# Moving transposed-tile copies from VectorE to ScalarE, joining two copies, and reordering the last pass of a transformer layer

## The reference

```
def _L0_attn_ref(src, ...):
    Q = elu(src @ Wq + bq) + 1 ;  K = elu(src @ Wk + bk) + 1 ;  v = src @ Wv + bv
    KV = einsum('bshd,bshm->bhdm', K, v)
    Z = 1.0 / (einsum('bshd,bhd->bsh', Q, K.sum(axis=1)) + EPS)
    o = einsum('bshd,bhdm,bsh->bshm', Q, KV, Z)
    x = LN(src + o @ Wo + bo, g1, be1)
    y = gelu(x @ W1 + b1) @ W2 + b2
    return LN(x + y, g2, be2)
def _L0_ffn_ref(x, weight, disha):
    pooled = x.reshape(..., 1024 // 64, 64).sum(axis=-2)
    return x @ weight.T + pooled @ disha
x = x + _L0_attn_ref(LN(x), ...)
x = x + _L0_ffn_ref(LN(x), weight, disha)
```

## Time and profile before

| what | value |
|---|---|
| runs shown | 2300.01 and 2508.72 us, median 2404.36 us |
| profiled execution, its time | 2298.4 us |
| profiled execution, span of its slowest core (core 2) | 2296.9 us |
| spans of the eight cores | 2281.9 to 2296.9 us |
| granted clock of TensorE, mean of each core | 0.903 to 0.907 |
| busy: PE, DVE, ACT, POOL | 1867.8, 687.0, 697.9, 218.3 us |

### The profile page before, as it was taken

The page is one execution under the profiler, slowest core; times in us unless marked ns, Lnnn a source line. Parts: engine busy times, 40 slices in busy tenths (PEclk is TensorE's granted clock), DMA queues, the critical chain, the costliest instruction groups (busy, mean ns, idle before and its releaser), DMA issues.

```text
span 2296.9 us, 36221 instructions; the slowest of 8 cores (2281.9 to 2296.9 us)
## 1 busy us (share of the span) xinstructions
PE 1867.8 (81%) x12660; PEld 1109.0 (48%) x12850; DVE 687.0 (30%) x1115; ACT 697.9 (30%) x1326; POOL 218.3 (10%) x186
## 2 busy tenths in 40 slices
PE   3888878887857777499999999999999999477766
PEld 1444444444433333266666666666666666343333
DVE  2232333333237777400000000000000000376674
ACT  1333333333323333223222222222222222233222
POOL 6000000000002222200000000000000000222220
PEclk9999999998978888699999999999999999777777
DMA  9930111111026665401112111110111110245542
GB/s 181 183 89 29 55 38 47 37 47 38 10 84 191 199 184 170 117 24 52 52 51 51 51 51 47 47 25 26 44 47 47 47 47 29 101 149 200 184 165 101
DMA packets 64084, 191.41 MB, mean 83 GB/s; under 512 B 7907, under 2 KB 8036, under 8 KB 62884
## 3 DMA queue, kind: packets, MB, share of 16 engines
q1 hardware_dynamic: 29108, 94.55, 12.6%
q0 software_dynamic: 16368, 35.80, 10.2%
q10 hardware_dynamic: 18432, 58.73, 6.6%
HBM read 166.12 MB, written 58.72 MB: 98 GB/s over the span
## 4 chain that ended last, share of the span: by engine, by line
PE 40%; DVE 13%; DMA 8%; issue 5%; ACT 2%; DVEq 0%; ACTq 0%; SPq 0%; POOL 0%; POOLq 0%
PE psC L920 19%; DVE arena L209 13%; PE psA L932 10%; PE psB L932 10%; DMA arena<-u_s 5%; DMA x_s<-arena 3%; ACT arena L209 2%; PE psB L702 1%; DMA arena<-Wf 0%; PE psA L947 0%; PE psA L1260 0%; DVEq L208 0%; PE psC L1260 0%; DMA arena<-x 0%; ACTq L1034 0%
## 5 line engine op out<-in xcount | busy, mean ns | idle before, releaser
L920 PE MATMUL psC<-arena 128*128 128x256 bf16 x4096 | 540.1, 277 | 18.0 <-DVE arena L209 18.0
L920 PEld LDWEIGHTS psC<-arena 128*128 128x128 bf16 x4096 | 405.2, 99 | 175.7 <-issue 23.8
L209 DVE SCALAR_TENSOR_TENSOR arena<-psA,arena 128x256 bf16<-128x256 f32 (+2 forms) x160 | 93.6, 585 | 1218.4 <-PE psA L947 945.9
L209 ACT ACTIVATE arena<-psC,arena 128x256 bf16<-128x256 f32 x512 | 242.3, 473 | 635.0 <-PE psC L920 629.8
L209 ACT ACTIVATE arena<-arena 128x1 f32<-128x1 f32 (+3 forms) x418 | 248.8, 595 | 350.2 <-DVE arena L209 314.4
L932 PE MATMUL psA<-arena 128*128 128x512 bf16 x960 | 294.3, 383 | 37.0 <-ACT arena L209 34.2
L932 PE MATMUL psB<-arena 128*128 128x512 bf16 x976 | 297.4, 383 | 2.5
L209 DVE SCALAR_TENSOR_TENSOR arena<-arena 128x1024 f32<-128x1024 f32 (+1 forms) x128 | 172.3, 1346 | 104.0 <-DMA arena<-u_s 37.1
L209 DVE TENSOR_SCALAR arena<-arena 128x1 f32<-128x1 f32 (+1 forms) x322 | 179.5, 557 | 73.6 <-ACT arena L209 30.6
L932 PEld LDWEIGHTS psB<-arena 128*128 128x128 bf16 x1024 | 101.0, 99 | 124.2 <-issue 6.0
L554 PE MATMUL psA<-arena 128*128 128x256 bf16 x1024 | 151.1, 297 | 0.0
(11 more groups left out here) (111 smaller groups left out, 1438.3 us busy)
## 6 DMA issues: line engine op xcount, KB each, us to landing
arena<-x SPq DMA_DIRECT2D x96, 512.0 KB, 5.4
x_s<-arena ACTq DMA_DIRECT2D x32, 512.0 KB, 3.9
arena<-x_s SPq DMA_DIRECT2D x32, 512.0 KB, 7.8
u_s<-arena ACTq DMA_DIRECT2D x32, 512.0 KB, 8.6
arena<-u_s SPq DMA_DIRECT2D x32, 512.0 KB, 5.3
out<-arena ACTq DMA_DIRECT2D x32, 512.0 KB, 6.0
arena<-W POOLq DMA_DIRECT2D x32, 256.0 KB, 74.2
qt_s<-arena ACTq DMA_DIRECT2D x32, 256.0 KB, 2.3
```

Of the source, the lines that this page charges most:

```text
L209: inst = fn(*a, **kw)
L920: ii = te.matmul(ph, w1_v[w][:, c * P:(c + 1) * P], x1t[:, w, :], start=(w == 0), stop=(w == NCH - 1))
```

## The change

It has three parts. In pass B1 the two half copies of `sc_VoT` become one of 1024 columns, and `pe_Pat` waits for it before its first matmul. In pass B2a the two copies `cvxt` leave DVE and go to ACT as `scxt`, ahead of and behind `scw`, with the same waits; DVE keeps only `cvu`. In pass B2b `vcols` of a pair is run one pair later, behind that pair's `vg2`, `vout` goes ahead of `vn`, and `ar3` on ACT goes to the head of the next pair.

```diff
@@ pass B1, PE and ACT
-                    W(te, f"bVoTa_{u}")
+                    W(te, f"bVoT_{u}")
...
-                        if w == 4:
-                            W(te, f"bVoT_{u}")
...
-                    sc.copy(oTv[:, 0:512], ps_bf[:, 0:512],
-                            key=f"bVoTa_{u}")
-                    sc.copy(oTv[:, 512:1024], ps_bf[:, 512:1024],
-                            key=f"bVoT_{u}")
+                    sc.copy(oTv[:, :], ps_bf[:, :], key=f"bVoT_{u}")
@@ pass B2a, DVE
                 for st in range(NSUP):
                     if st >= 1:
                         cvu(2 * st - 2)
-                    cvxt(2 * st)
-                    cvxt(2 * st + 1)
-                    if st >= 1:
                         cvu(2 * st - 1)
@@ pass B2a, ACT
+                def scxt(t):
...
+                    sc.copy(x1tv[:, :, sub * P:(sub + 1) * P],
+                            pt.rearrange("p (c s) -> p c s", c=NCH),
+                            key=f"cVxT_{t}")
...
                 for st in range(NSUP):
+                    scxt(2 * st)
                     scw(st)
+                    scxt(2 * st + 1)
                     for c in range(NFCH):
@@ pass B2b, DVE
                     vg2(t)
                     vg2(t2)
                     if p >= 1:
-                        vn(t - 2)
-                        vn(t2 - 2)
+                        vcols(t - 2)
+                        vcols(t2 - 2)
                     if p >= 2:
                         vout(t - 4)
                         vout(t2 - 4)
+                    if p >= 1:
+                        vn(t - 2)
+                        vn(t2 - 2)
                     vxa(t)
                     vxa(t2)
-                    vcols(t)
-                    vcols(t2)
+                vcols(T - 2)
+                vcols(T - 1)
@@ pass B2b, ACT
                     if p >= 1:
+                        ar3(t - 2)
+                        ar3(t2 - 2)
                         nT_(t - 2)
...
                     sq(t)
                     sq(t2)
-                    ar3(t)
-                    ar3(t2)
+                ar3(T - 2)
+                ar3(T - 1)
```

More of the change, by code:

```diff
@@ L957, in _ @@
                 psDbf_v = psD.ap().bitcast(BF16)
-                def cvxt(t):
-                    if t >= T:
-                        return
-                    st = t // 2
-                    sub = t % 2
-                    pt = ps_bf[:, :] if sub == 0 else psDbf_v[:, 0:1024]
-                    W(v, f"cPt_{t}")
-                    W(v, f"cPh_{st - 2}_{NFCH - 1}")
-                    x1tv = x1Ts if st % 2 == 0 else x1Ts2
-                    v.tensor_copy(x1tv[:, :, sub * P:(sub + 1) * P],
-                                  pt.rearrange("p (c s) -> p c s", c=NCH),
-                                  key=f"cVxT_{t}")
                 def cvw(st):
@@ L1014, in scw @@
                                 key=f"cVW_{st}")
+                def scxt(t):
+                    st_ = t // 2
+                    sub = t % 2
+                    pt = ps_bf[:, :] if sub == 0 else psDbf_s[:, 0:1024]
+                    W(sc, f"cPt_{t}")
+                    W(sc, f"cPh_{st_ - 2}_{NFCH - 1}")
+                    x1tv = x1Ts if st_ % 2 == 0 else x1Ts2
+                    sc.copy(x1tv[:, :, sub * P:(sub + 1) * P],
+                            pt.rearrange("p (c s) -> p c s", c=NCH),
+                            key=f"cVxT_{t}")
+                psDbf_s = psD.ap().bitcast(BF16)
                 for st in range(NSUP):
+                    scxt(2 * st)
                     scw(st)
+                    scxt(2 * st + 1)
                     for c in range(NFCH):
```

## The result

The kernel with the change is slower: 1.0251 times the time before, with a 95% interval of 1.0236 to 1.0266, some 58 us. The forecast was 2350 us, 1.022 times the profiled execution before. The medians of all executions, 2447.08 us of 11 with the change and 2303.89 of 10 before, contain, for both kernels, disturbed ones, in which the cores of a die show a lower clock; every ratio here leaves them out, and the other executions of the change lie between 2357.07 and 2360.03 us. The profiled execution took 2360.35 us, 62 more than the one before.

The account below looks back on a forecast made before the run. PE was taken to bound pass B2a, and a ring of DVE work, an SP issue and a DMA pass B2b. B1 0, B2a +55 and B2b -3 gave +52 us on 2298.4: 2350 us, range 2320 to 2385.

Parts of the forecast that it names:

- my number stands against the former: Whole kernel: the forecast is to be compared with the run at 2300.01 us, not the one at 2508.72.
- the clock term: Pass B2a: lower PE clock after longer stops at 15 meetings, 25 us against 13 before: +12, bounds 0 and 25.
- B1, 0 us: Pass B1, joined copies: PE's later start is covered, as DVE doesn't wait for this product: 0 us, from -8 to +14.
- the upper bound of 14 us: Pass B1: PE's first matmul starts 0.43 us later, 32 times, with nothing covering it.
- The waiting term: Pass B2a: `py` 2.35 us later at eight meetings, 3.3 at seven with a weight piece: 42 us.
- Eight matmuls take half of 1.91 us: Pass B2a, meetings: time of the first `ph` products after the stop, leading to `py` at about +9.1.
- the +80 of the pass: Pass B2a together: upper bound of the forecast of +55 us, from +43 to +80.
- B2b, -3 us: Pass B2b, reordering: a pair goes from 17.6 to 17.4 us, over 15 pairs -3 us, from -27 to +22.
- rival 1: Pass B2b: reordering pays fully, pairs fall to 15.8 us, -27 us, B2a's clock no worse: 2314 us; chance 0.20.
- PE's ring: Pass B2b: PE from transposition to last product, plus `vout` and `vn`: no pair can be under 15.8 us.
- Rival 2: Pass B2b: loads gain nothing and column operations take their full price, +22 us: 2375 us; chance 0.22.
- Rival 3: Pass B2a: copies hidden behind PE, the meetings cost nothing: 2295 us, or 2271 with rival 1's gain; chance 0.03.

Follow-up runs that it names:

- run 2: Kernel before with only the change's B2a part, the copies moved to ACT: 2361.65 us, ratio 1.0259 to the kernel before.
- run 4: Whole change, but on ACT the copies of the next super tile stand ahead of the two squares and stores: 2319.65 us, 1.0076 to the kernel before.
- run 7: The change's B1 and B2b, but B2a's copies stay on DVE, behind both `cvu`: 2301.39 us, 0.9994 to the kernel before.
- Run 1: Kernel before with only the change's B1 part, the joined copy: 2306.94 us, ratio 1.0014 to the kernel before.
- run 5: Whole change, with PE's stops at B2a's meetings filled by matmuls whose product nobody reads: 2331 to 2345 us, 1.0164 to the kernel before.
- Run 3: Kernel before with only the change's B2b part, the new order: 2302.72 us, ratio 1.0003 to the kernel before.
- run 6: Whole change, with the square of the mean in `vcols` as TENSOR_SCALAR instead of TENSOR_TENSOR: 2355.57 us, 1.0238 to the kernel before.
- run 10: run 9 with the change's B2b order and the column product of run 6: 2223.31 us, 0.9663 to the kernel before.
- run 9: Kernel before, B2a's transpositions and squares moved inside super tiles, B2b's u loads issued ahead of x loads: 2221.79 us, 0.9657 to the kernel before.
- run 11: run 9 without POOL's addition of be2, which is left out of the output: 2157.15 us, 0.9373 to the kernel before.
- run 12: run 9 with be2 added by DVE instead of POOL, a complete kernel: 2186.35 and 2192.27 us.

## Where the prediction failed, and what of it held

**The time.** The step that failed is "my number stands against the former". It set the sum on 2298.4 us and the range, 2320 to 2385, around it, and put at nothing what sets the median of all executions apart. That median is 2447.08 us, 62 above the end of the range and some 89 above the 2358 us to which the sum is an answer. No run takes these 89 us apart, and their cause stays open.

**The mechanism.** Against 2358 us the forecast of 2350 is 8 us short; 1.022 against 1.0251. The cause is the one named: the copies stand behind both squares and stores in ACT's queue. Runs 2, 4 and 7 show it from three sides. Of the 8 us, 4 are the clock term and 4 pass B2b (below).

**B1, 0 us: held, within the noise.** Run 1 gives 1.0014, from -4 to +11 us, so the upper bound of 14 us is excluded only just. The wait that was to show it hardly moved (5.1 us in the earlier trace rows):

```profile
DVE arena L209 <- PE psB L705: 5.9, 1, 5.9
```

**B2a, the steps.** Forecast from the first `cvu`: first copy +4.86, `ph` +7.2; measured +4.88 and +7.25. With a weight piece `ph` was put at +9.2 and came at +9.53. The waiting term was 42 us and measured 42.8 (run 5): 3.3 against 3.3 with a weight piece, 2.5 against 2.35 without.

**B2a, `py`.** I had put it at +9.1 and, with a weight piece, +11.1, and in the trace it is at +10.4 and +12.7. The step that was wrong is "Eight matmuls take half of 1.91 us": I took the full clock for the first products after the stop, while the stretch at half clock begins inside the stop and takes in all of them (3.57 us). I had counted the clock as a term of its own, so the sum hardly suffers: at full clock, in run 5, `py` is at +9.4 and +11.1.

**The clock term** was 12 us with bounds 0 and 25, and it was too small: by the accounting of run 5 it is 16. One stretch at each of the 15 meetings was forecast and found. The total cost at the lower clock was put at 25 us and is 29; the 13 us for the kernel before were right. (The upper bound is a slip: twice as long over work would be 50 - 13 = +37, which is what the +80 of the pass goes by, not +25.)

**B2b, -3 us.** Run 3 gives +0.7 us, from -2 to +3: the term was some 4 us too good. Its steps held: stores 4.0 us behind `vxa` (4.1 forecast), u in 5.5 us (5.4), `vg2` blocked for 0.95 us (1.0), the column product at 2.16 us (2.15), `vn` at 0.81 us, and pairs of 17.0 to 17.4 us on the eight cores (17.4), counted over the last 13. Two things were off. The 17.59 us that I started from is one pair of core 2, whose mean is 17.7, while the other seven cores had 17.2 to 17.4; over the eight cores the 15 pairs together gained 1.4 us and not 3. And I put the end of the pass at nothing, where the later `vn` is not made up for: from the first `vxa` of the last pair to the end of the span the cores take 37.0 to 39.7 us before and 41.4 to 42.6 after, 3.4 us more in the mean. There PE starts on the second-last pair's product 3.5 us behind that `vxa` (core 7, 2319.72 and 2316.19), where it was 1.1 us (core 2, 2259.44 and 2258.38), and the last `vout` and `vn` wait for it. Of rival 1, PE's ring, there is a sign only in run 6, once the block was off the column product. Rival 2 fell with u landing in 5.5 us. Rival 3 fell with run 2; run 7 shows the piece of truth in it, a delay of 1.35 us of which a part is hidden by the squares.

**Not settled.** Of run 10 I can say only that DVE waits there for stores (37.3 us) and for `psC` (29.6 us). Whether a different order of stores would free it was not tried.

## What to carry to other kernels

When work moves to a less busy engine, read where in that engine's queue it lands: a copy on which PE waits must stand ahead of work that nobody waits for, and the idle share of the engine says nothing about it. Better still is to take the hand-over out of the place where everything waits: PE's transpositions for the next tile belong in the middle of this one. And price GpSimd's additions by what they block on VectorE, not by their own length.

## What was not expected

- A stop of PE of 2.0 us was followed by the lower clock at only three of the eight later meetings before (those super tiles take 63.8 to 63.9 us, the others 61.8 to 62.2), one of 6.2 us at every one, and it then held for 3.5 us of work. Products that nobody reads, put in the stops, kept the clock at 1.00 and made the pass 28 us and the kernel some 20 us faster.
- The 32 additions on POOL, 2.3 to 3.2 us each in run 9, on an engine with nothing else to do there, cost 64 us of a kernel of 2222 us (runs 9 and 11), about twice the 29 to 35 us that they cost on DVE (run 12), the busiest engine of that pass.
- A block by POOL hits a DVE operation on one column as hard as one on 1024: 2.16 us against its 0.16 us alone. With the column as its scalar operand it is not blocked.
